# Group statistics moved into the filter network, and their rows kept in SBUF: one conv, attention and feed-forward block on one core

## The chip, the cores and the metric

The kernel runs on one core of one Trainium2 chip. The metric is the device time of one execution in microseconds (us), lower is better. The kernel before takes 5605.55 us, the median of three runs (5603.51 to 5610.34).

## The reference

Input x is 8 images of 56x56 tokens with 256 channels, float32. The block is a long-convolution layer, a linear attention and a feed-forward layer with a Haar transform. What this change touches is the front of the first layer:

```python
def _gn(v, G=32, eps=1e-05):              # group norm, 32 groups of 8 channels
    g = v.reshape(B_, H_, W_, G, C_ // G)
    m = jnp.mean(g, axis=(1, 2, 4), keepdims=True)
    s = jnp.var(g, axis=(1, 2, 4), keepdims=True)
    return ((g - m) / jnp.sqrt(s + eps)).reshape(v.shape)

def rpe_coeffs(...):                      # filter taps: a small network over 111 x 111 offsets
    t = coords @ rpe_in_w.T + rpe_in_b
    for i in range(3):
        t = relu(simple_rms(t)) @ rpe_h_w[i].T + rpe_h_b[i]
    return relu(simple_rms(t)) @ rpe_out_w.T + rpe_out_b

def _L0_conv_ref(x, ...):                 # called with _gn(x)
    shortcut = x
    xn = simple_rms(x)
    u, v = silu(xn @ W_u.T + b_u), silu(xn @ W_v.T + b_v)
    y = irfft2(rfft2(v) * rfft2(filter))
    return (u * y) @ W_o.T + b_o + shortcut

x = x + _L0_conv_ref(_gn(x), ...)
```

The filter does not depend on x, and the statistics of x (a mean and a variance for each image and group) do not depend on the filter.

## The kernel before, in words

The program is a row of phases. Each is a `Tools` block that owns its SBUF and PSUM tiles and semaphores and ends with a barrier of all engines (L149 to L153); the next phase's loads are issued only behind it. In a phase every engine has its own hand-written list of instructions, in the order of the code, and the engines meet at semaphores. SyncE (SP) issues the loads and stores. Tiles carry the phase's prefix: kr, st, pr, co, mx, at, ff.

**Filter network** (kernel_rows_phase, kr). All constants are loaded first, among them `coords`, 6 x 12544; TensorE, VectorE, ScalarE and GpSimd wait for all eleven loads, and TensorE for all four weight splits besides. Then come 14 steps of two halves u = 0, 1, each of four rows of offsets (448 points). A step has layers numbered n = 0 to 7 (n = 2 * layer + u). `deeper_layer` (TensorE) is six products, the block `mean` of 16 small matmuls for the layer before (L266), six products, and two bias products (L289). ScalarE squares (L348), rectifies (L352) and takes the root (L358); VectorE makes the low parts (`low_parts`, L429) and the scale rows (`next_scale`, L408 to L422). The tail of a step is eight rows m: output products, `kr_coef` (VectorE, L446), and `row_pass` (TensorE, L297) into the two PSUM banks `kr_row_ps`, which ScalarE copies out (L370). GpSimd only copies the points of the next step out of `coords` (L243).

**Statistics** (stats_phase, st). The 56 chunks of x (448 tokens each, tile 112 x 4 x 256) are loaded, turned by eight TensorE transposes (L797) into PSUM and measured by two VectorE bn_stats (L853). After each image come the two group means (L775, L779), the normalisers, four spreading matmuls that copy scale and shift along a row (L786), and a copy and seven stores that write the row of 512 values to `gn_rows` in DRAM, once for each chunk.

**Projection** (project_phase, pr). GpSimd clears four x tiles; then SP loads, for each chunk, two halves of x (56 rows x 4 KB each) and the chunk's row of `gn_rows`, broadcast to 128 partitions (256 KB). GpSimd multiplies and adds (L973, L976, `pr_gx`); ScalarE takes squares; TensorE turns (`front`, L993), projects (L135) and does the row transform (L1013). TensorE waits for all constants before the first `front`.

**Columns** (co) does the column transforms and is not touched. **Mix** (mix_phase, mx) loads x and the `gn_rows` row (224 KB) again for each chunk, and GpSimd again normalises (L1350, L1352) before TensorE turns the result (L1384). Attention (at) and feed-forward (ff) follow, untouched.

Of the kernel before, what the change touches and what calls it, by code (L numbers as in the profile page):

```python
# [165 lines left out]
def kernel_rows_phase(nc, d):  # L166

    with Tools(nc, "kr") as T:  # L170
# [14 lines left out]
        coords = T.sb("coords", [6, TAPS_PAD * TAPS_PAD])  # L185
# [9 lines left out]
        rows_out = [T.sb(f"rows_out{u}", [ROWS, RPE_ROWS, WIDE]) for u in range(2)]  # L195
        t_ps = [T.ps(f"t{u}", [128, 1024]) for u in range(2)]
# [4 lines left out]
        (consts_in, high_consts, low_consts, points_ready, layer_done, high_ready, low_ready, squared, mean_done, rooted,  # L201
         scaled, scale_split, scale_mixed, scale_ready, column_mm, inverted, coef_mm, coef_done, row_mm, row_out) = (T.sem(n) for n in (
             "consts_in", "high_consts", "low_consts", "points_ready", "layer_done", "high_ready", "low_ready", "squared",
# [8 lines left out]
        loads = [(raw_in, "rpe_in"), (coords, "coords"), (low_rows, "low_rows"), (own_row, "own_row"), (mean_ch, "mean_ch"),  # L212
                 (raw_h, "rpe_h"), (raw_bias, "rpe_bias"), (raw_out, "rpe_out"), (ident, "ident"), (out_bias, "rpe_out_b"),
                 (row_taps, "row_taps")]
# [9 lines left out]
        with nc.Block() as block:  # L224
            @block.sync
            def _(sp):
                for tile, name in loads:
                    sp.dma_start(tile[:], d[name]).then_inc(consts_in, 16)
                with sp.Fori(0, STEPS) as s:
                    for u in range(2):  # L230

                        sp.wait_ge(row_out, s * TAIL + RPE_ROWS * (u + 1))
                        sp.dma_start(d["kern_rows"][:, bass.ds((s * 2 + u) * RPE_ROWS, RPE_ROWS), :],
                                     rows_out[u][:]).then_inc(stored[u], 16)
# [4 lines left out]
            def _(pool):  # L239
                pool.wait_ge(consts_in, 16 * len(loads))  # L240

                def take_points(s, u):
                    nc.gpsimd.tensor_copy(points[u][:], coords[:, bass.ds((s * 2 + u) * RPE_CHUNK, RPE_CHUNK)]  # L243
                                          ).then_inc(points_ready, 1)

                for u in range(2):
                    take_points(0, u)
                with pool.Fori(1, STEPS) as s:
                    for u in range(2):
                        pool.wait_ge(layer_done, s * PER + (u + 1 - PER))  # L250
# [618 lines left out]
def project_phase(nc, d):  # L869

    with Tools(nc, "pr") as T:
# [52 lines left out]
        with nc.Block() as block:  # L924
            @block.sync
            def _(sp):
# [17 lines left out]
                for j in range(GROUP):  # L944
                    load(0, j)
# [1694 lines left out]
```

## Time and profile before

| what | value |
|---|---|
| median of three runs | 5605.55 us |
| the profiled execution | 5614.06 us, its span 5612.2 us |
| TensorE matmul | busy 5297.2 us, 94% of the span |
| VectorE | 3942.1 us, 70% |
| ScalarE | 2461.5 us, 44% |
| GpSimd | 2495.2 us, 44% |
| moved by DMA | 810.15 MB, mean 144 GB/s |
| mean granted clock of TensorE | 0.968 of full speed |

The profiled execution is 8.5 us above the median of the runs. The page of the profile gives busy time by engine and by fortieth of the span; the answers of the trace give single instructions with their start and duration (timeline), and sums over a stretch (windows). A matmul's end is modelled, so the pace of TensorE is read from start to start. The second row of the page's slices has TensorE below nine tenths in the first, fifth and sixth slices, where the phases kr, st and pr begin, and again at the later phase borders.

### The profile page before, as it was taken

How to read it: one execution, taken by the hardware profiler on the slowest of the kernel's cores; microseconds unless marked ns; L12 is line 12 of the kernel's file. 1: busy time of each engine (PE TensorE's matmuls, PEld its weight loads, DVE VectorE, ACT ScalarE, POOL GpSimd, SP SyncE). 2: the span in 40 equal slices, each digit the busy share in tenths (PEclk: the TensorE clock that was granted, in tenths of full speed). 3: DMA queues.
4: the chain of work that ended last, by engine and by line, in shares of the span. 5: the costliest groups of instructions: out<-in, count | busy, mean ns of one | idle time of the engine just before them, and what ended most of it. 6: DMA issues, size and time to landing. Idle time of an engine off the chain costs nothing. (4 is left out here: it accounts for less than half of the span.)

```text
span 5612.2 us, 90234 instructions
## 1 busy us (share of the span) xinstructions
PE 5297.2 (94%) x26964; PEld 3688.4 (66%) x26964; DVE 3942.1 (70%) x6109; ACT 2461.5 (44%) x4685; POOL 2495.2 (44%) x1385
## 2 busy tenths in 40 slices
PE   8999869998999999999998999999799999987999
PEld 5667545554555555555556777777676666665999
DVE  4555556665899999999995666676545555555787
ACT  4444238786334343443333555555532222210555
POOL 0000024442899999999995555555201111111332
PEclk9999879999999999999999999999899999997999
DMA  1111568887444444444446666666523333322443
GB/s 44 39 52 40 139 165 245 242 243 219 143 149 151 151 148 152 147 151 150 149 135 188 208 209 213 206 217 204 163 86 101 102 97 104 102 82 82 120 123 113
DMA packets 364270, 810.15 MB, mean 144 GB/s; under 512 B 45135, under 2 KB 149507, under 8 KB 354618
## 3 DMA queue, kind: packets, MB, share of 16 engines
q1 hardware_dynamic: 341648, 731.51, 44.3%
q10 hardware_dynamic: 22512, 77.20, 3.6%
q8 instruction: 66, 1.08, 0.1%
q14 instruction: 44, 0.36, 0.0%
HBM read 448.08 MB, written 360.49 MB: 144 GB/s over the span
## 5 line engine op out<-in xcount | busy, mean ns | idle before, releaser
L717 POOL TENSOR_TENSOR co_prod<-co_cross 111x512 f32<-111x512 f32 x448 | 850.2, 1898 | 0.0
L651 ACT ACTIVATE co_y_out<-co_y_ps 112x512 f32<-112x512 f32 x448 | 267.9, 598 | 927.6 <-PE co_y_ps L597 922.8
L714 POOL TENSOR_TENSOR co_prod<-co_direct 111x512 f32<-111x512 f32 x448 | 577.4, 1289 | 202.1 <-PE co_y_ps L597 115.4
L691 DVE TENSOR_TENSOR co_direct<-co_v_ps,co_spec 111x1024 f32<-111x1024 f32 x448 | 543.3, 1213 | 92.3 <-PE co_v_ps L135 87.8
L1917 POOL TENSOR_TENSOR at_t<-at_t,at_p_bias 112x1024 f32<-112x1024 f32 x56 | 134.2, 2409 | 976.1 <-DMA at_t<-t_tiles 976.1
L693 DVE TENSOR_TENSOR co_cross<-co_v_ps,co_spec 111x1024 f32<-111x1024 f32 x448 | 541.3, 1208 | 0.0
L135 PE MATMUL co_v_ps<-co_v_high,co_col_fwd_high 112*111 112x512 f32 x896 | 506.1, 565 | 1.4 <-DVE co_cross L693 1.4
L595 PE MATMUL co_y_ps<-co_prod,co_col_inv 111*112 111x512 f32 x896 | 458.2, 592 | 0.0
L597 PE MATMUL co_y_ps<-co_prod,co_col_inv 111*112 111x512 f32 x896 | 457.5, 592 | 0.1
L671 DVE TENSOR_TENSOR co_v_low<-co_v_in,co_v_high 112x1024 fp32r<-112x1024 f32 x224 | 372.4, 1662 | 0.1
L2081 ACT ACTIVATE at_qk_t<-at_bank_ps 128x448 f32<-128x448 f32 x224 | 121.8, 544 | 567.9 <-PE at_bank_ps L135 567.8
L135 PE MATMUL co_v_ps<-co_v_low,co_col_fwd_high 112*111 112x512 f32 x896 | 354.3, 395 | 0.0
L135 PE MATMUL co_v_ps<-co_v_high,co_col_fwd_low 112*111 112x512 f32 x896 | 349.2, 390 | 0.0
L1512 ACT ACTIVATE mx_mixed_high<-mx_turn_ps 128x448 fp32r<-128x448 f32 x224 | 122.0, 544 | 430.7 <-PE mx_turn_ps L1413 430.7
L597 PEld LDWEIGHTS co_y_ps<-co_prod,co_col_inv 111*112 111x112 f32 x896 | 156.0, 175 | 229.4 <-issue 212.3
L1148 DVE SCALAR_TENSOR_TENSOR pr_v_pre<-pr_v_ps,pr_inv,pr_v_bias 120x512 f32<-120x512 f32 x224 | 167.6, 748 | 155.9 <-PE pr_v_ps L135 150.6
L973 POOL TENSOR_TENSOR pr_gx<-pr_x_in,pr_gn 128x1024 f32<-128x1024 f32 x56 | 135.4, 2418 | 312.1 <-DMA pr_gn<-gn_rows 267.8
L2402 POOL TENSOR_TENSOR ff_base<-ff_t,ff_n 112x1024 f32<-112x1024 f32 x56 | 132.8, 2371 | 312.2 <-DVE ff_out L2563 280.9
L135 PE MATMUL mx_o_ps<-mx_w_o_high,mx_mixed_high 128*112 128x256 f32 x896 | 252.3, 282 | 3.5 <-DVE mx_mixed_low L1630 3.5
L135 PE MATMUL mx_o_ps<-mx_w_o_high,mx_mixed_low 128*112 128x256 f32 x896 | 252.1, 281 | 0.0
L243 POOL CAST kr_points<-kr_coords 6x448 fp32r (+1 forms) x28 | 15.6, 558 | 530.5 <-PE kr_t_ps L274 511.9
L135 PE MATMUL mx_o_ps<-mx_w_o_low,mx_mixed_high 128*112 128x256 f32 x896 | 250.7, 280 | 0.0
(267 smaller groups left out, 14107.8 us busy)
## 6 DMA issues: line engine op xcount, KB each, us to landing
v_rows<-pr_rows_out SPq DMA_DIRECT2D x56, 1792.0 KB
co_v_in<-v_rows SPq DMA_DIRECT2D x448, 224.0 KB
y_rows<-co_y_out SPq DMA_DIRECT2D x448, 224.0 KB
mx_y_in<-y_rows SPq DMA_DIRECT2D x224, 448.0 KB, 5.5
kern_rows<-kr_rows_out SPq DMA_DIRECT2D x28, 896.0 KB
st_x_in<-x SPq DMA_DIRECT2D x56, 448.0 KB, 11.4
pr_x_in<-x SPq DMA_DIRECT2D x112, 224.0 KB
mx_x_in<-x SPq DMA_DIRECT2D x56, 448.0 KB, 4.8
```

The source lines that it names most:

```text
L135: last = nc.tensor.matmul(out, weights[a], data[b], start=start and i == 0, stop=stop and i == len(passes) - 1)
L595: nc.tensor.matmul(y_ps[b % 2][:2 * SIDE, :], col_inv[:, 0, :], prod[b % 2][:, :WIDE], start=True, stop=False)
L597: nc.tensor.matmul(y_ps[b % 2][:2 * SIDE, :], col_inv[:, 1, :], prod[b % 2][:, WIDE:], start=False, stop=True).then_inc(inv_mm, 1)
L651: nc.scalar.activation(y_out[:, b, :], y_ps[b % 2][:2 * SIDE, :], ACT.Copy).then_inc(y_ready, 1)
L671: nc.vector.tensor_tensor(v[1][:, images, :], v_in[:, images, :], v[0][:, images, :].bitcast(F32), ALU.subtract).then_inc(low_v, 1)
L691: nc.vector.tensor_tensor(direct[b % 2][:], v_ps[b % 2][:POINTS, :], spec[i][:, :2 * WIDE], ALU.mult).then_inc(real_terms, 1)
L693: nc.vector.tensor_tensor(cross[b % 2][:], v_ps[b % 2][:POINTS, :], spec[i][:, WIDE:], ALU.mult).then_inc(multiplied, 1)
L714: nc.gpsimd.tensor_tensor(prod[b % 2][:, :WIDE], direct[b % 2][:, :WIDE], direct[b % 2][:, WIDE:], ALU.subtract).then_inc(real_ready, 1)
L717: nc.gpsimd.tensor_tensor(prod[b % 2][:, WIDE:], cross[b % 2][:, :WIDE], cross[b % 2][:, WIDE:], ALU.add).then_inc(combined, 1)
L973: nc.gpsimd.tensor_tensor(gx[j][:], x_in[j][:], gn[j][:, 0:1, :].to_broadcast([128, TILES, CH]), ALU.mult).then_inc(scaled, 1)
L1148: nc.vector.scalar_tensor_tensor(out=v_pre[t % 2][:], in0=v_ps[t % 2][:SPAN, :], scalar=inv[:SPAN, j % GROUP * TILES + t:j % GROUP * TILES ...
L1917: nc.gpsimd.tensor_tensor(t1[j % HELD][:], t1[j % HELD][:], p_bias[:].unsqueeze(1).to_broadcast([TILE, TILES, CH]), ALU.add).then_inc(t1_b ...
```

## The change

* stats_phase is gone. Its loads, transposes and bn_stats stand in the kr phase: five chunks a step, one behind each of the layers n = 2 to 6, in steps 0 to 10, the 56th chunk in step 11. They use the banks `kr_row_ps`, which the tail of the step uses otherwise. The aggregates are made in the tail of step 11, the group means and normalisers in step 12 for all images at once, and the spreading matmuls and copies of the eight rows in steps 12 and 13.
* `gn_rows` is an SBUF tile, 128 x 8 x 512, that lives from kr to mix. The DRAM tensor, its 56 stores and its 112 broadcast loads are gone.
* The points come in pieces of 6 x 448, two a step. The constants of kr are in three groups with a semaphore each (inputs, weights, tail), and each engine waits only for the group that it needs.
* In pr the first two chunks are loaded ahead of the constants, each as soon as its own tile is cleared; VectorE normalises chunk 0, GpSimd the others; ScalarE splits the weights and copies chunk 0 before it takes the squares of chunk 1; VectorE makes the first low part before the inverse.
* In mix the first x chunk is loaded ahead of the constants, and GpSimd does not wait for these to normalise.
* Loops: kr on TensorE, ScalarE and VectorE loops over 11 steps and has 3 written out (13 and 1 before); kr on SP and GpSimd, and the normalising on GpSimd in pr and mix, are written out in full.

```diff
-def kernel_rows_phase(nc, d):
+def kernel_rows_phase(nc, d, gn_rows):
+    PER_STEP = 5
-        coords = T.sb("coords", [6, TAPS_PAD * TAPS_PAD])
+        group_mean = T.sb("group_mean", [128, 128])
+        coords = [T.sb(f"coords{u}", [6, RPE_CHUNK]) for u in range(2)]
+        x_in = [T.sb(f"x_in{i}", [TILE, TILES, CH]) for i in range(PER_STEP)]
...
+        input_loads = [(raw_in, "rpe_in"), (low_rows, "low_rows")]
+        weight_loads = [(raw_h, "rpe_h"), (mean_ch, "mean_ch"), (raw_bias, "rpe_bias"), (own_row, "own_row"), (ident, "ident")]
+        tail_loads = [(raw_out, "rpe_out"), (out_bias, "rpe_out_b"), (row_taps, "row_taps"), (group_mean, "group_mean")]
+        X_LOOP = X_CHUNKS // PER_STEP
...
+                def load_x(s, i):
+                    if s:
+                        sp.wait_ge(turned, (s - 1) * PER_STEP + i + 1)
+                    sp.dma_start(x_in[i][:], d["x_tiles"][s * PER_STEP + i]).then_inc(x_loaded[i], 16)
...
+                def turn_chunk(s, i):
+                    pe.wait_ge(x_loaded[i], s * 16 + 16)
+                    if i:
+                        pe.wait_ge(measured, s * PER_STEP + i)
+                    if i < 2:
+                        pe.wait_ge(row_out, s * TAIL)
+                    for h in range(HALVES):
+                        for t in range(TILES):
+                            last = nc.tensor.transpose(row_ps[h][:, t * TILE:(t + 1) * TILE], x_in[i][:, t, h * 128:(h + 1) * 128],
+                                                       ident[:TILE, :TILE])
+                    last.then_inc(turned, 1)
...
                     for n in range(2, PER):
                         deeper_layer(s, n)
+                        between_layers(s, n)
...
                     for n in range(1, PER):
                         low_parts(s, n)
+                        between_layers(s, n)
                         next_scale(s, n)
...
+                def take_rows(b):
+                    dve.wait_ge(gn_mm, b + 1)
+                    nc.vector.tensor_copy(gn_rows[:, b, :], row_ps[b % 2][:]).then_inc(gn_ready, 1)
...
-def stats_phase(nc, d):
...
-                    sp.dma_start(gn[j][:].rearrange("p a c -> p (a c)"), d["gn_rows"][GROUP * s + j].to_broadcast([128, 2 * CH])
-                                 ).then_inc(loaded[j], 16)
...
-                sp.wait_ge(cleared, GROUP)
-                for j in range(GROUP):
+                for j in range(2):
+                    sp.wait_ge(cleared, j + 1)
                     load(0, j)
                 for tile, name in loads:
                     sp.dma_start(tile[:], d[name]).then_inc(consts_in, 16)
+                for j in range(2, GROUP):
+                    sp.wait_ge(cleared, j + 1)
+                    load(0, j)
...
+                dve.wait_ge(loaded[0], 32)
+                nc.vector.tensor_tensor(gx[0][:], x_in[0][:], scale0, ALU.mult).then_inc(scaled0, 1)
+                dve.wait_ge(scaled0, 1)
+                nc.vector.tensor_tensor(gx[0][:], gx[0][:], shift0, ALU.add).then_inc(gx_ready, 1)
```

TensorE at the end of layer n = 2 of a kr step, before (kr_t0_ps belongs to half 0; the two bias products end the layer):

```order
L135 MATMUL kr_t0_ps<-kr_rect0_high,kr_w_h_low 128x448
L287 ISA
L289 MATMUL kr_t0_ps<-kr_scale_rows0,kr_bias_rows_both 128x448 x2
L280 ISA
L135 MATMUL kr_t1_ps<-kr_rect1_high,kr_w_h_high 128x448
```

and after:

```order
L135 MATMUL kr_t0_ps<-kr_rect0_high,kr_w_h_low 128x448
L386 ISA
L388 MATMUL kr_t0_ps<-kr_scale_rows0,kr_bias_rows_both 128x448 x2
L309 ISA
L316 MATMUL kr_row0_ps<-kr_ident,kr_x_in0 128x112 x4
L316 MATMUL kr_row1_ps<-kr_ident,kr_x_in0 128x112 x4
L379 ISA
L135 MATMUL kr_t1_ps<-kr_rect1_high,kr_w_h_high 128x448
```

The eight transposes of one chunk stand between the bias products of one layer and the first product of the next.

VectorE around the same layer, after; before, the same rows stood there without the BN_STATS and their ISA rows:

```order
L541 SCALAR_TENSOR_TENSOR kr_rect_low<-kr_t_ps,kr_rect_high 128x448
L549 ISA
L557 ISA
L557 BN_STATS kr_stats<-kr_row_ps 128x6
L557 ISA
L557 BN_STATS kr_stats<-kr_row_ps 128x6
L513 REGISTER_ALU
L522 SCALAR_TENSOR_TENSOR kr_scale<-kr_scale,kr_root 128x112
L527 CAST kr_scale_high<-kr_scale 128x112
L528 REGISTER_ALU
L529 SCALAR_TENSOR_TENSOR kr_scale_both<-kr_scale_high,kr_low_rows,kr_scale 128x112
L534 TENSOR_TENSOR kr_scale_rows<-kr_scale_both,kr_own_row 128x448
```

The two bn_stats stand between the low parts and the scale of a layer.

VectorE at the start of pr, before:

```order
L1176 TENSOR_TENSOR pr_w_v_low<-pr_raw_v,pr_w_v_high 128x1024
L1178 TENSOR_SCALAR pr_guarded<-pr_root 128x8
L1180 RECIPROCAL pr_inv<-pr_guarded 128x8
L1140 TENSOR_TENSOR pr_x_t_low<-pr_xt_ps,pr_x_t_high 128x480 x2
L1148 SCALAR_TENSOR_TENSOR pr_v_pre<-pr_v_ps,pr_inv,pr_v_bias 120x512 x2
```

and after:

```order
L1207 TENSOR_TENSOR pr_gx<-pr_x_in,gn_rows 128x1024
L1209 TENSOR_TENSOR pr_gx<-pr_gx,gn_rows 128x1024
L1211 TENSOR_TENSOR pr_w_v_low<-pr_raw_v,pr_w_v_high 128x1024
L1170 TENSOR_TENSOR pr_x_t_low<-pr_xt_ps,pr_x_t_high 128x480 x2
L1214 TENSOR_SCALAR pr_guarded<-pr_root 128x8
L1216 RECIPROCAL pr_inv<-pr_guarded 128x8
L1178 SCALAR_TENSOR_TENSOR pr_v_pre<-pr_v_ps,pr_inv,pr_v_bias 120x512 x2
```

Two operations on chunk 0 come first, and the low part of the turned chunk no longer stands behind the inverse.

## Rows read from the trace of the kernel before

**Rows 1.** Windows: stretch, us, busy us (count) by engine, clock, DMA share, GB/s.
```profile
45.00:630.70 585.70, 582.83 (x3813) 402.19 (x3811) 323.37 (x702) 284.04 (x540) 13.43 (x24) 1.00 0.13 42
641.00:760.50 119.50, 81.38 (x544) 68.89 (x544) 80.29 (x192) 1.62 (x8) 0.00 (x0) 0.80 0.95 210
800.00:1380.00 580.00, 579.87 (x2646) 343.61 (x2644) 380.86 (x607) 460.08 (x1057) 243.78 (x102) 1.00 0.79 237
```

**Rows 2.** Timeline (start us, duration us, instruction, idle before): borders of the st phase.
```profile
636.09 0.37 SPq L757 DMA_DIRECT2D st_ident<-ident  x1
...
641.09 3.30 PE L797 MATMUL st_x_ps<-st_ident,st_x_in 112*128 112x112 f32 x16 [11.47 <-DMA st_x_in<-x]
...
760.54 3.62 POOL L965 MEMSET pr_x_in<- 128x1024 f32 x4 [214.03 <-POOLq L153]
```

**Rows 3.** Timeline: one layer of a kr step.
```profile
554.25 0.35 PEld L266 LDWEIGHTS kr_ms_ps<-kr_square,kr_mean_ch 128*32 128x32 f32 x16 [0.30 <-ACT kr_square L348]
...
554.53 1.16 DVE L429 SCALAR_TENSOR_TENSOR kr_rect_low<-kr_t_ps,kr_rect_high 128x448 fp32r<-128x448 f32 x2 [0.87 <-ACT kr_rect_high L352]
...
555.60 0.27 DVE L410 SCALAR_TENSOR_TENSOR kr_scale<-kr_scale,kr_root 128x112 f32<-128x112 f32 x1
...
556.53 0.62 DVE L422 TENSOR_TENSOR kr_scale_rows<-kr_scale_both,kr_own_row 128x448 fp32r<-128x448 f32 x1
...
557.80 0.35 PEld L266 LDWEIGHTS kr_ms_ps<-kr_square,kr_mean_ch 128*32 128x32 f32 x16 [0.30 <-ACT kr_square L348]
```

**Rows 4.** Timeline of TensorE: a turned chunk and a spread row in st.
```profile
663.69 0.98 PE L797 MATMUL st_x_ps<-st_ident,st_x_in 112*128 112x112 f32 x8 [0.96 <-DMA st_x_in<-x]
664.51 0.65 PE L786 MATMUL st_row_ps<-st_ident,st_scale 128*128 128x128 f32 x4
...
665.54 0.98 PE L797 MATMUL st_x_ps<-st_ident,st_x_in 112*128 112x112 f32 x8
```

**Rows 5.** Timeline of TensorE: a turned chunk inside a full stream, in pr.
```profile
1005.95 1.04 PE L993 MATMUL pr_xt_ps<-pr_ident,pr_gx 120*128 120x120 f32 x8
1006.75 0.47 PE L135 MATMUL pr_v_ps<-pr_w_v_high,pr_x_t_high 128*120 128x512 f32 x1
```

**Rows 6.** The tile st_stats: duration ns min/median/max, first and last start.
```profile
L853 DVE BATCH_NORM_STATS2 st_stats<-st_x_ps x112: 612/616/633, 642.9 to 748.1; 128x6 f32<-128x448 f32 x112
```

**Rows 7.** Timeline: start of the kr phase.
```profile
18.98 0.41 ACT L340 ACTIVATE kr_w_in_high<-kr_raw_in 6x256 fp32r<-6x256 f32 x1 [16.95 <-DMA kr_row_taps<-row_taps]
...
21.41 1.04 ACT L343 ACTIVATE kr_w_out_high<-kr_raw_out 128x1024 fp32r<-128x1024 f32 x1
...
25.84 0.92 ACT L348 ACTIVATE kr_square<-kr_t_ps 128x896 f32<-128x896 f32 x1 [3.39 <-PE kr_t_ps L274]
...
28.75 0.74 PE L135 MATMUL kr_t_ps<-kr_rect_high,kr_w_h_high 128*128 128x448 f32 x1
```

**Rows 8.** DMA between 14 and 19 us.
```profile
DMA packets 294, 0.33 MB, mean 65 GB/s; under 512 B 129, under 2 KB 177, under 8 KB 294
```

**Rows 9.** Timeline: start of the pr phase.
```profile
771.31 2.34 POOL L973 TENSOR_TENSOR pr_gx<-pr_x_in,pr_gn 128x1024 f32<-128x1024 f32 x1 [7.16 <-DMA pr_gn<-gn_rows]
...
782.97 1.06 ACT L1111 ACTIVATE pr_w_v_high<-pr_raw_v 128x1024 fp32r<-128x1024 f32 x1 [0.20 <-DMA pr_ident<-ident]
...
784.06 2.56 DVE L1176 TENSOR_TENSOR pr_w_v_low<-pr_raw_v,pr_w_v_high 128x1024 fp32r<-128x1024 f32 x1 [28.08 <-ACT pr_w_v_high L1111]
...
790.43 0.75 PE L135 MATMUL pr_v_ps<-pr_w_v_high,pr_x_t_high 128*120 128x512 f32 x1 [5.58 <-issue]
```

**Rows 10.** Timeline: start of the mx phase.
```profile
2969.33 1.23 DVE L1722 TENSOR_TENSOR mx_w_u_low<-mx_raw_u,mx_w_u_high 128x1024 fp32r<-128x1024 f32 x1 [6.20 <-ACT mx_w_u_high L1592]
...
2981.28 2.37 POOL L1350 TENSOR_TENSOR mx_gx<-mx_x_in,mx_gn 112x1024 f32<-112x1024 f32 x1 [4.88 <-DMA mx_gn<-gn_rows]
...
2986.40 0.93 PE L1384 MATMUL mx_turn_ps<-mx_ident,mx_gx 112*128 112x112 f32 x4
```

**Rows 11.** Timeline of TensorE in st: a chunk turned at the lower clock.
```profile
671.29 1.75 PE L797 MATMUL st_x_ps<-st_ident,st_x_in 112*128 112x112 f32 x8 [0.42 <-DMA st_x_in<-x]
```

More of the change, by code:

```diff
@@ L239, in _ @@
             def _(pool):
[L240 removed]
                 def take_points(s, u):
[L243 to L248, printed above, removed]
+                    pool.wait_ge(coords_in[u], 16 * (s + 1))
+                    if s:
+                        pool.wait_ge(layer_done, s * PER + (u + 1 - PER))
+                    nc.gpsimd.tensor_copy(points[u][:], coords[u][:]).then_inc(points_ready, 1)
+                for s in range(STEPS):
                     for u in range(2):
[L250 removed]
                         take_points(s, u)
@@ new lines, in spread_rows @@
+                def spread_rows(b):
+                    pe.wait_ge(chain, SHIFT)
+                    if b >= 2:
+                        pe.wait_ge(gn_ready, b - 1)
+                        pe.wait_ge(row_out, (X_LOOP + 2) * TAIL)
+                    for i, col in enumerate((gn_scale, gn_shift)):
+                        for h in range(HALVES):
+                            at = (i * HALVES + h) * 128
+                            last = nc.tensor.matmul(row_ps[b % 2][:, at:at + 128], col[:, h, b:b + 1].to_broadcast([128, 128]),
+                                                    ident[:], start=True, stop=True)
+                    last.then_inc(gn_mm, 1)
@@ L1356, in residual @@
                     pool.wait_ge(gx_ready, g + 1)
-                    if not first:
+                    if first:
+                        pool.wait_ge(consts_in, 16 * (len(loads) + 2))
+                    else:
                         pool.wait_ge(t1_ready, s * 4 + (u - 1) * 2 + SLOTS)
@@ L1368, in _ @@
                 residual(0, 1, first=True)
-                with pool.Fori(1, PAIRS - 1) as s:
+                for s in range(1, PAIRS - 1):
                     normalise(s, 1)
@@ L2584, in program @@
     scratch("kern_rows", (ROWS, TAPS_PAD, WIDE))
-    scratch("gn_rows", (chunks, 1, 2 * CH))
     scratch("inv_cols", (chunks // 2, 128, 2 * TILES))
@@ L2598, in program @@
     d["out"] = d["result"].rearrange(flat).rearrange("(g t p) c -> g p t c", t=TILES, p=TILE)
-    for phase in (kernel_rows_phase, stats_phase, project_phase, columns_phase, mix_phase, attention_phase, ffn_phase):
-        phase(nc, d)
+    with nc.sbuf_tensor("gn_rows", [128, BATCH, 2 * CH], F32) as gn_rows:
+        kernel_rows_phase(nc, d, gn_rows)
+        project_phase(nc, d, gn_rows)
+        columns_phase(nc, d)
+        mix_phase(nc, d, gn_rows)
+    attention_phase(nc, d)
+    ffn_phase(nc, d)
 def kernel(**inputs):
```

346 lines of the change are left out of this document (170 added, 176 removed).

## The prediction

> **What bounds the kernel now.** I read the slices of the page first, to find where TensorE is not full, then windows over the stages that the change touches, then the timeline at their borders. The windows [rows 1] show three different cases. In kr TensorE is busy 582.83 of 585.70 us at full clock (2.4 GHz), while VectorE works 323 us and the DMA engines 13% of the time: TensorE sets the pace, and the DMA queues and nearly half of VectorE are free. In st it is the other way round: DMA share 0.95 at 210 GB/s, TensorE 81 of 119.5 us and mostly waiting for the next chunk (the row of [rows 2] at 641.09 waits for `st_x_in`). In pr TensorE is full again, 579.87 of 580, at full clock. So the change takes a stretch bound by loads and puts it under a stretch bound by TensorE. The loads become free there, the transposes do not.
>
> **The statistics phase goes.** Its first instruction is at 636.09 us and the next phase's first at 760.54 [rows 2], the one SP's first load and the other GpSimd's first clear behind the same kind of barrier. That is 124.4 us off, with a barrier, the waiting for the first load, the closing chain of normalisers and the stores of `gn_rows` all inside.
>
> **What TensorE gets in kr.** Turning a chunk takes 0.82 us from start to start (663.69 to 664.51, [rows 4]), in a full stream 0.80 with 120 columns instead of 112 [rows 5]. Changing from products to another kind of matmul costs something too: the block of means has 0.30 us of idle weight loading before it [rows 3], and between bias products and next layer there is no such change today. No row shows this very change, so I bound it by 0 and by 0.5 us a chunk (such a gap on entering and some of one on leaving), and take 0.2, nearer to the lower end because pr has the same change without a visible loss: 1.0 us x 56 chunks = 56 us (45 to 73). A spread row takes 1.03 us (664.51 to 665.54, [rows 4]), eight of them 8.2 us; two group means, each no longer than the half of such a row, 1 us. Together 65 us, all on the path, since TensorE is full.
>
> **What VectorE gets in kr.** A layer lasts 3.55 us on TensorE (554.25 to 557.80, [rows 3]) and becomes 4.55 us. VectorE has 1.16 us of low parts and 1.55 us of scale work in it (555.60 to the end of 556.53 + 0.62, [rows 3]), and gets 2 x 0.616 us of bn_stats [rows 6]: 3.94 of 4.55 us, so it should still fit. Behind the bn_stats stand the scale, the next low parts and the next bias product, which have about a layer of slack. The tight one is the new wait: the next chunk may be turned only when the last one is measured, since both use the same two banks. Low parts start about 1.4 us after a layer's last product (554.53 is 0.28 behind the block of means, which has six products ahead of it), end at 2.6, the bn_stats at about 3.9, and the next turn is due at 4.55. Slack 0.6 us: no cost. The copies of the rows (one a layer) and the aggregates in the tail are smaller than a chunk's bn_stats and hide the same way. ScalarE gets one small root.
>
> **Queues.** SP now waits for a turned chunk before each x load, and the stores of `kern_rows` stand behind these waits. The last chunk of a step is turned at n = 6, and the store waits for a row of the tail anyway, so nothing is late. Each x load has a whole step before it is needed, some 45 us, where a load lands within 5 us (636.09 to 641.09, two small constants included, [rows 2]). Points have at least as long. GpSimd's copies are two small ones a step. All of this costs nothing; if a load were late, TensorE would wait for it in the turn.
>
> **Start of kr.** Now everything lands at 18.98 us, ScalarE splits the four weights, the last of them at 21.41, the first square is at 25.84 and the first deep product at 28.75 [rows 7], 9.8 us after landing. After the change only the last split (1.04 us) stands between the landing of the tail group and the first square, since the first layer is done by then; from square to product stays 2.91 us. That is 4.1 us after landing instead of 9.8: 5.7 us saved. When the tail lands is open: between 14 and 19 us only 0.33 MB moved, in small packets at 65 GB/s [rows 8], and the row tables that are last now are still in the last group. I take 1.2 us earlier for the 294 KB of coordinates that left the queue (bounds: 0.5 later, 5 earlier). Sum 6.9 us (5 to 11).
>
> **Start of pr.** The weights and constants land at 782.97, behind four chunks with their broadcast rows, and products start at 790.43 [rows 9]. By the shapes the queue carried 4 x 704 KB + 0.9 MB from the end of the clears (760.54 + 3.62, [rows 2]) on, in 18.8 us, about 200 GB/s. After: two chunks of 448 KB and 0.9 MB, 9 us, and the queue starts 2.7 us earlier because it waits for one of the four clears: constants at about 771. Then turn, copy, low part, about 4.7 us: products at 776.0, 14 us earlier. The new work on VectorE is two passes over 128 x 1024. The same kind of pass took 1.23 us with GpSimd idle [rows 10] and 2.56 us beside GpSimd [rows 9], so 2.5 to 5.1 us, and it ends before the constants land either way if chunk 0 lands in 5 us. The range of this term is 10 to 16 us.
>
> **Rest of pr, and mix.** The broadcast loads that go were beside a full TensorE: nothing. At the start of mix, TensorE turns the second chunk at 2986.40, right behind GpSimd's work on it, which began at 2981.28 when its row had landed [rows 10]. 448 KB less in front of it are 2 us at the 210 GB/s of [rows 1]. The first products come some 4 us earlier, but then wait for that chunk: 2 us (0 to 4).
>
> **Sum.** -124.4 + 65 - 6.9 - 14 - 2 = -82 us. The profiled execution took 5614 us and would take 5532; the median of the runs is 8.5 us lower, so 5523.5 us. About 0.2% (11 us) is what a measurement of this kernel can tell from no change.
>
> **A rule against the change.** The windows with transposes show both levels of the clock: pr, which turns a chunk between its products, has 1.00, and st, where TensorE waits between chunks, has 0.80; there a chunk's eight transposes took 1.75 us at one place [rows 11] and 0.98 at another [rows 4]. The Trainium skill ("TensorE: Matmul & The Clock Gate", Part 4: PE-mode transpose) says that transpose mode does not count as busy for the clock in the way that matmuls do. By that rule five interruptions a step could cost kr its full clock (the third rival below); the full clock of pr speaks against it for short groups.
>
> **The rivals.**
> * *VectorE or the two banks set the pace.* If the register work and waits around the bn_stats, which no row shows, eat the slack, TensorE waits for `measured` before each turn. With 5.1 us a layer that is 0.55 x 55 = 30 us more, 5554 us. If turn and bn_stats stood wholly in line, 1.23 x 56 = 69 us more, 5592 us. For it: 0.6 us of slack in a hand-timed chain. Against it: 3.94 of 4.55. 10%.
> * *The starts give little.* The tail of small packets stays and GpSimd holds VectorE in pr: 8 us instead of 23, 5538 us. 9%, inside the range.
> * *Slower: the clock falls in kr.* Place: the eleven steps with chunks. Price: a step is 43 us (28.75 to 630.7 in 14) and would take up to twice that at 1.2 GHz, 43 us each; from two steps on it eats the 82 us, all eleven would make it 6000 us. For it: st's 0.80 [rows 1]. Against: in st TensorE idled a third of the time, in kr it will not. 3%.
> * *The statistics are not hidden at all* (loads too late, turns waiting for DMA): as in the first rival; 1%, since the queue is at 13%.
>
> **How the numbers follow.** The forecast, 5523.5 us, has 77%, with a range of its own of 5503 (turns at 0.8 us, starts at their best) to 5548 us (turns at 1.3 us, starts at their worst). That holds the second rival and part of the first, so it is the range. Faster by over 0.2% is everything but the clock and the fully serial case: 0.95; within 0.2%, 0.02; slower 0.03.
>
> **What would show it.** The first clear of pr should come at about 636 + 65 - 7 = 694 us, with TensorE full at clock 1.00 up to there; a step with chunks 5 us longer than 43; turns without idle time before them released by `kr_stats`; DMA near 130 GB/s there. Products of pr should start 15 to 17 us after its first clear, not 30. Wrong would be: a TensorE wait on the bn_stats in kr, a clock below 1.00 there, or steps of over 51 us.

## The result, and the profile after

The changed kernel takes 5512.68 us (median of 4 runs, 5506.79 to 5516.2), the kernel before 5606.46 us on the same chip (4 runs, 5603.51 to 5610.34): ratio 0.9837, 95% interval 0.9824 to 0.9849, so 94 us faster. The forecast was 5523.5 us in a range of 5503 to 5548. The profiled execution took 5516.2 us with a span of 5514.4 us, against 5532 forecast for it. The page of the changed kernel, busy time by engine, then TensorE and its granted clock in 40 slices:

```profile
PE 5263.6 (95%) x26936; PEld 3667.2 (67%) x26936; DVE 3927.7 (71%) x6061; ACT 2458.8 (45%) x4678; POOL 2490.1 (45%) x1383
...
PE   8999899997999999999989999999799999987999
...
PEclk9999999998999999999999999999899999998999
```

The first window of the next view is the stretch of the kr phase with chunks in it, the second its end (columns as in [rows 1]):

```profile
45.00:570.00 525.00, 521.29 (x3587) 370.65 (x3585) 324.48 (x693) 237.31 (x450) 11.62 (x22) 1.00 0.26 80
570.00:676.00 106.00, 105.18 (x675) 73.69 (x673) 59.89 (x136) 46.47 (x88) 1.06 (x2) 1.00 0.14 44
```

TensorE is as full as in [rows 1], at clock 1.00 in both windows, and the DMA share has only doubled. So the statistics are hidden behind TensorE in all but their transposes. The timeline of one layer shows how (start us, duration us, instruction):

```profile
311.24 0.59 PE L365 MATMUL kr_ms_ps<-kr_square,kr_mean_ch 128*32 128x112 f32 x16
...
311.88 1.15 DVE L557 BATCH_NORM_STATS2 kr_stats<-kr_row_ps 128x448 f32 x2
...
312.95 0.26 DVE L522 SCALAR_TENSOR_TENSOR kr_scale<-kr_scale,kr_root 128x112 f32<-128x112 f32 x1
...
313.08 0.57 PE L388 MATMUL kr_t_ps<-kr_scale_rows,kr_bias_rows_both 128*128 128x448 f32 x2
...
313.48 0.93 PE L316 MATMUL kr_row_ps<-kr_ident,kr_x_in 112*128 112x112 f32 x8
...
314.19 0.45 PE L135 MATMUL kr_t_ps<-kr_rect_high,kr_w_h_high 128*128 128x448 f32 x1
...
315.58 0.47 PE L365 MATMUL kr_ms_ps<-kr_square,kr_mean_ch 128*32 128x112 f32 x9
```

A layer with a chunk goes from 311.24 to 315.58, 4.34 us; without one it was 3.55 [rows 3]. In none of the 56 turns does TensorE stand idle before it. The last chunk's bn_stats end at 313.03, 0.45 us before the next turn at 313.48.

The border of the phases and the start of pr, from the timeline (idle time before in brackets):

```profile
681.98 3.62 POOL L995 MEMSET pr_x_in<- 128x1024 f32 x4 [92.23 <-POOLq L153]
...
687.32 1.22 DVE L1207 TENSOR_TENSOR pr_gx<-pr_x_in,gn_rows 128x1024 f32<-128x1024 f32 x1 [13.31 <-DMA pr_x_in<-x]
688.58 1.22 DVE L1209 TENSOR_TENSOR pr_gx<-pr_gx,gn_rows 128x1024 f32<-128x1024 f32 x1
...
692.15 1.06 ACT L1139 ACTIVATE pr_w_v_high<-pr_raw_v 128x1024 fp32r<-128x1024 f32 x1 [0.60 <-DMA pr_ident<-ident]
...
693.24 2.33 DVE L1211 TENSOR_TENSOR pr_w_v_low<-pr_raw_v,pr_w_v_high 128x1024 fp32r<-128x1024 f32 x1 [3.43 <-ACT pr_w_v_high L1139]
...
696.80 0.75 PE L135 MATMUL pr_v_ps<-pr_w_v_high,pr_x_t_high 128*120 128x512 f32 x1 [2.77 <-issue]
```

pr begins at 681.98 instead of 760.54 [rows 2], 78.6 us earlier. Its first product comes 14.8 us after that instead of 29.9 [rows 9]. Then the gap between the two kernels stays the same for 3200 us: 93.6 us at pr's first product, 94.1 us at the last product `mx_u_ps` of mix. The other 3.7 us of the span's 97.8 come behind mix, where the code is unchanged.

The start of kr (timeline):

```profile
17.05 1.06 ACT L452 ACTIVATE kr_w_out_high<-kr_raw_out 128x1024 fp32r<-128x1024 f32 x1 [5.93 <-DMA kr_group_mean<-group_mean]
18.01 0.90 ACT L457 ACTIVATE kr_square<-kr_t_ps 128x896 f32<-128x896 f32 x1
...
21.00 0.74 PE L135 MATMUL kr_t_ps<-kr_rect_high,kr_w_h_high 128*128 128x448 f32 x1
```

The first deep product is at 21.00 instead of 28.75 [rows 7]. So the kr phase from its first deep product to pr's first clear grew by 124.45 + 7.75 - 78.56 = 53.6 us.

### The profile page after: what moved, and what is told of

It is laid out like the page before. It is cut to its first block and busy times, and to the rows that moved or that the text cites. A ratio compares the mean times of both kernels' runs of the same rounds, so it can differ in the third digit from the quotient of the medians.

```text
span 5514.4 us, 88804 instructions
## 1 busy us (share of the span) xinstructions
PE 5263.6 (95%) x26936; PEld 3667.2 (67%) x26936; DVE 3927.7 (71%) x6061; ACT 2458.8 (45%) x4678; POOL 2490.1 (45%) x1383
## 5 line engine op out<-in xcount | busy, mean ns | idle before, releaser
L1395 POOL TENSOR_TENSOR mx_resid<-mx_x_in,mx_o_bias 112x1024 f32<-112x1024 f32 x56 | 133.2, 2379 | 319.0 <-DVE mx_t L1677 319.0
L297 POOL CAST kr_points<-kr_coords 6x448 fp32r<-6x448 f32 x28 | 15.0, 558 | 574.3 <-DMA kr_coords<-coords 574.3
L1005 POOL TENSOR_TENSOR pr_gx<-pr_x_in,gn_rows 128x1024 f32<-128x1024 f32 x55 | 133.3, 2424 | 300.0 <-DMA pr_x_in<-x 299.9
```

## The experiments

Eleven kernels ran, each the changed kernel with one edit, or several where said. Where only a span is given, it is that of a single execution; three of the kernels were run 4 or 5 times. "Deep product" is the first product of a deeper layer in kr, "clear" the first clear that opens pr or mix.

**What a chunk costs TensorE.** The forecast had 0.2 us a chunk for changing to transposes and back.

```
-                        for t in range(TILES):
+                        for t in range(TILES // 2):
                             last = nc.tensor.transpose(row_ps[h][...
-                        last = nc.vector.bn_stats(at[h], row_ps[h][:, :CHUNK])
+                        last = nc.vector.bn_stats(at[h], row_ps[h][:, :CHUNK // 2])
```

Half of the points are left out of the statistics here.

> Leaves out half of the statistics: only four of a chunk's eight transposes, and bn_stats over 224 of 448 columns, so the statistics are those of half the tokens. A step with five chunks lasts 46.98 us in the changed kernel and 42.86 before: 0.82 us a chunk. Theory A (a transpose costs its own columns and entering and leaving transposes costs nothing): 0.41 us a chunk, a step of 44.9 us, kr 23 us shorter. Theory B (my 0.2 us of switching is there, and the transposes are cheaper than I took them): 0.2 + 0.31 us a chunk, a step of 45.4 us.

Span 5485.1 us (time 5486.89). The timeline of TensorE in two successive layers, blocks of means, bias products and turns:

```profile
301.02 0.59 PE L365 MATMUL kr_ms_ps<-kr_square,kr_mean_ch 128*32 128x112 f32 x16
...
302.87 0.57 PE L388 MATMUL kr_t_ps<-kr_scale_rows,kr_bias_rows_both 128*128 128x448 f32 x2
...
303.27 0.55 PE L316 MATMUL kr_row_ps<-kr_ident,kr_x_in 112*128 112x112 f32 x4
...
304.99 0.59 PE L365 MATMUL kr_ms_ps<-kr_square,kr_mean_ch 128*32 128x112 f32 x16
```

A layer takes 3.97 us, against 4.34 with eight transposes and 3.55 with none [rows 3]: 0.42 us for the first four, 0.37 for the next four. A fixed price for the change of kind would leave the first four much dearer; 0.05 us is left for it. By whole steps it is nearly the same: 45.10 us here, 46.98 in the changed kernel, 42.86 before, so 0.45 us a chunk for the first half and 0.38 for the second, with 0.07 left. The price of a chunk is that of its eight transposes, 0.82 us by whole steps, with the change of kind in it. Theory A had 44.9 us for the step, theory B 45.4; 45.10 lies between them, nearer to A.

**Whether VectorE has slack.** Each bn_stats is made twice, the first into a tile that nobody reads:

```
                     for h in range(HALVES):
+                        nc.vector.bn_stats(spare[:, h, :], row_ps[h][:, :CHUNK])
                         last = nc.vector.bn_stats(at[h], row_ps[h][:, :CHUNK])
```

> Each chunk is measured twice (four bn_stats instead of two, the first two into a spare tile), 1.23 us more for VectorE in each layer with a chunk: 5.2 us of work in a layer of 4.34. Theory (VectorE has 0.4 to 0.6 us of slack a layer and TensorE waits for nothing but the banks): the next turn now waits for the measuring, a layer lasts 4.9 to 5.2 us, a step 50 to 51 us, kr 32 to 45 us longer, with TensorE idle ahead of the turns and kr_stats as the releaser. Rival (the slack of the low parts and the scale, about a layer, takes it up): a step of 47 to 48 us.

Span 5526.1 us (time 5527.92), a step 48.62 us: 1.6 us more in five layers, of 5.4 us more work. TensorE, blocks of means, and then VectorE in the same stretch:

```profile
330.94 0.59 PE L366 MATMUL kr_ms_ps<-kr_square,kr_mean_ch 128*32 128x112 f32 x16
...
333.46 0.78 PEld L317 LDWEIGHTS kr_row_ps<-kr_ident,kr_x_in 112*128 112x128 f32 x8 [0.49 <-DVE kr_stats L559]
333.46 0.98 PE L317 MATMUL kr_row_ps<-kr_ident,kr_x_in 112*128 112x112 f32 x8
...
335.61 0.59 PE L366 MATMUL kr_ms_ps<-kr_square,kr_mean_ch 128*32 128x112 f32 x16
```

```profile
330.12 1.16 DVE L542 SCALAR_TENSOR_TENSOR kr_rect_low<-kr_t_ps,kr_rect_high 128x448 fp32r<-128x448 f32 x2
331.19 0.62 DVE L558 BATCH_NORM_STATS2 kr_spare<-kr_row_ps 128x6 f32<-128x448 f32 x1
331.73 0.61 DVE L559 BATCH_NORM_STATS2 kr_stats<-kr_row_ps 128x448 f32 x1
...
334.78 1.15 DVE L542 SCALAR_TENSOR_TENSOR kr_rect_low<-kr_t_ps,kr_rect_high 128x448 fp32r<-128x448 f32 x2
```

VectorE now works without a gap and its cycle is 4.66 us (330.12 to 334.78), which is also TensorE's layer (330.94 to 335.61, 4.67). One bn_stats costs 0.54 us from start to start, so without the two extra ones the cycle is 3.6 us of work against a layer of 4.34. The weight load of the turn waits for `kr_stats`, as the theory said: 55 of the 56 turns do so here, 30.8 us in all, and none in the changed kernel. So the wait for the banks, the forecast's first rival, exists and begins to cost once VectorE's work exceeds the layer. Neither expectation hit the size (steps of 50 to 51 or 47 to 48 us): there is slack of 0.7 us a layer, 0.3 of the 1.07 us doubled does not fit.

**The start of kr.** In the next kernel everything waits for the last load, as in the kernel before, the coordinates still loaded by the step:

```
 def _(pe):
+    pe.wait_ge(inputs_in, ...)
+    pe.wait_ge(weights_in, ...)
+    pe.wait_ge(tail_in, ...)
+    pe.wait_ge(low_consts, 4)
-    pe.wait_ge(low_consts, 1)
```

and likewise for ScalarE and GpSimd.

> The changed kernel, but in kr TensorE, VectorE, ScalarE and GpSimd wait for all three groups of constants (TensorE for the four splits too) before anything else, as before the change; the points still come by the step. First deep product: 21.0 us in the changed kernel, 28.75 before. Theory (5.7 us are the splits and the first layer done ahead, 2 us the coordinates that left the queue): 26.8 us. Rival (the smaller load is all of it): 21 to 22 us. Other rival (only the grouping counts): 28.5 us. The rest of kr keeps its length.

Deep product at 27.7 us instead of 21.0, pr's clear at 688.3 instead of 682.0: 6.3 to 6.7 us are the order of waits and splits, and the 1.1 us left to the kernel before (28.75) would be the smaller load. The theory had 26.8 us, the second rival 28.5. One run does not settle between them: in the eight kernels that have the changed kernel's start of kr the deep product came at 19.3 to 21.2 us. With this old order it came at 27.5 to 27.7 in two kernels, so most of the saving is the order. The span was 5513.0, no longer than the changed kernel's, mostly because mix and attention, untouched by the edit, took 1.6 and 5.1 us less in this run; the last section has the spread of attention. That is why the phase borders are compared here and not the ends.

The opposite edit goes further: no engine waits for the tail group before the w_out products of step 0, and the bias and w_h splits stand where they are first needed.

```
-                pe.wait_ge(tail_in, 16 * len(tail_loads))
-                pe.wait_ge(low_consts, 4)
+                pe.wait_ge(low_consts, 3)
                 over_steps(pe, step)
...
+                    if isinstance(s, int) and s == 0:
+                        pe.wait_ge(tail_in, 16 * len(tail_loads))
+                        pe.wait_ge(low_consts, 4)
                     for m in range(TAIL):
```

> One step further than the change: in kr the squares, rectified and low parts of the first layer are made before the weights land, TensorE starts the deep layers as soon as the weights group is split, and the output weights (tail group, landing at 17.0 us) are split only in the sixth layer of step 0, which is written out. Theory: weights land at 8.9 us, two splits in line are 3.4 us: first deep product at 12.5 us instead of 21.0, and the first clear of pr 8.5 us earlier. Rival (step 0 then waits for its x chunks or for the tail group): the deep product comes at 12.5 us, but TensorE stands idle later in step 0 and less than 4 us are left.

```profile
12.85 1.11 PE L374 MATMUL kr_t_ps<-kr_points,kr_w_in_both 6*128 6x448 f32 x2 [3.33 <-DVE kr_bias_rows_both L631]
13.88 0.74 PE L135 MATMUL kr_t_ps<-kr_rect_high,kr_w_h_high 128*128 128x448 f32 x1
```

Deep product at 13.9, pr's clear 8.1 us earlier (673.9), span 5503.6 (time 5505.42). So in the changed kernel the wait for the tail group and the splits before the first square still stood on the path, with 7.1 us by this pair of profiles and 5.4 to 7.3 against the 19.3 to 21.2 us above. Both texts had 12.5 us for the deep product; TensorE did not lose the gain again later in step 0, as the rival said.

**The start of pr.** The order of the kernel before is put back (all four clears, then all four chunks, then the constants; GpSimd normalises chunk 0), while the rows stay on chip:

```
-                for j in range(2):
-                    sp.wait_ge(cleared, j + 1)
-                    load(0, j)
+                sp.wait_ge(cleared, GROUP)
+                for j in range(GROUP):
+                    load(0, j)
                 for tile, name in loads:
```

> The changed kernel with the start of pr in its old order: SP waits for all four clears, loads four chunks and then the constants, GpSimd normalises chunk 0 too, ScalarE and VectorE have their old order. The broadcast loads stay away. In the changed kernel the first product of pr starts 14.8 us after the first clear (29.9 before). Theory (order of loads and work): constants now lie behind four chunks of 448 KB instead of two, so the first product comes 27 us after the first clear (2.5 us less than before, for the 1 MB of broadcast loads at 200 GB/s would be 5, of which the chain through GpSimd takes back half), and the whole kernel takes 12 us more. Rival (the missing broadcast loads are what saved it): the first product comes at 16 to 18 us, 2 us more at most.

```profile
697.80 1.86 PE L1017 MATMUL pr_xt_ps<-pr_ident,pr_gx 120*128 120x120 f32 x8 [24.32 <-DMA pr_ident<-ident]
...
699.63 1.04 ACT L1135 ACTIVATE pr_w_v_high<-pr_raw_v 128x1024 fp32r<-128x1024 f32 x1
...
700.70 2.87 DVE L1200 TENSOR_TENSOR pr_w_v_low<-pr_raw_v,pr_w_v_high 128x1024 fp32r<-128x1024 f32 x1 [28.39 <-ACT pr_w_v_high L1135]
703.50 2.30 DVE L1202 TENSOR_SCALAR pr_guarded<-pr_root 128x8 f32<-128x8 f32 x1
...
707.39 0.75 PE L135 MATMUL pr_v_ps<-pr_w_v_high,pr_x_t_high 128*120 128x512 f32 x1 [7.73 <-issue]
```

The clear was at 680.3, the first product 27.1 us later; the theory had 27. The later loads are the larger part of it: the constants were there 17.5 us after the clear (first turn, 697.80) instead of 10.2, which is 7.3 of the 12.3 us. The other 5.0 lie behind them: ScalarE splits w_v only after the squares of two chunks, and VectorE makes the low part only after the guard, which took 2.30 us beside GpSimd. The edit moves loads, chunk 0 and the order of work on two engines at once, and no run separates these. Of the 15.1 us gained at this place 12.3 are thus the order (with chunk 0 on VectorE), and the 2.8 left are put down to the broadcast loads that left the queue; the next experiment measures these by themselves. pr itself takes 586 us from first to last product either way. Span 5523.1 (time 5524.87).

**The broadcast rows.** They are loaded again beside each chunk, in pr and in mix, with nobody reading them:

```
+                    sp.dma_start(gn[j][:]..., d["x_pairs"][GROUP * s + j].to_broadcast([128, 2 * CH])
+                                 ).then_inc(loaded[j], 16)
```

> The changed kernel with a broadcast load of 512 values for each chunk put back in pr (256 KB) and mix (224 KB), from x and unused, in the old places of the queue, and waited for. Theory (TensorE is full in both phases, the loads are hidden): the starts of pr and mix lose what lies in front of their constants and second chunk, 2 to 3 us in pr and 0 to 2 in mix; between starts and ends both phases keep their length to 1 us; the kernel takes 2 to 5 us more. Rival (keeping the rows on chip is worth more than its starts, by less traffic beside the stores): 10 us more or above, with longer steps in pr or mix.

5516.91 us (5512.26 to 5520.66; ratio 0.984, 0.982 to 0.986), not to be told from the changed kernel. pr's first product comes 2.0 us later after the clear, mix's 1.1 us, and pr's length stays (584.7 us). Keeping the rows on chip is worth what they cost in a start queue, 3 us in all, and nothing that these runs could show beside a full TensorE.

**The start of mix.** The order of before (weights, then each chunk with its inverse rows):

> The changed kernel with the start of mix in its old order: the constants ahead of the first x chunk, GpSimd waits for them. In the changed kernel the first product starts 18.3 us and the turn of the second chunk 24.5 us after the first clear of the phase; before 19.3 and 24.5. Theory (both are held by what the queue has to move before the second chunk, which is the same in either order): first product at 18 to 19.5 us, turn of the second chunk at 23 to 24.5 us, no loss, perhaps a gain of 1 us. Rival (the new order saved 2 us, and something else ate it): turn of the second chunk at 26 to 27 us.

First product 20.5 us after the clear instead of 18.3, turn of the second chunk at 25.6 instead of 24.5, and 1047.4 us from clear to last product instead of 1045.5; span 5517.8. The theory (18 to 19.5 and 23 to 24.5 us) missed both, the rival (26 to 27) is nearer. A single pair of runs does not prove it, but the other profiles have the same starts: in the seven kernels with the new order the first product came 17.3 to 18.5 us after the clear and the second turn at 22.1 to 24.5, in the three with the old one (this one, all three starts old, and the kernel before, which has the broadcast loads besides) 19.1 to 20.5 and 24.4 to 25.6. The first products do not overlap, so the new order gains about 1.7 us on the mean there, and about 1 us at the second turn. From clear to last product it is 1043.9 to 1047.0 against 1046.4 to 1047.4. In the changed kernel's own profile the second chunk is still late, turned 24.5 us after the clear as before ([rows 10] and 2961.9 for the clear). So I put both x chunks ahead of everything but the constants:

```
-                for u in range(2):
-                    if u:
-                        load_x(0, u, first=True)
-                    load_inv(0, u, first=True)
+                load_x(0, 1, first=True)
+                for u in range(2):
+                    load_inv(0, u, first=True)
```

> The changed kernel with one edit: in the mix phase both x chunks are loaded ahead of the first y and inverse rows (before, the second chunk stands behind ten other loads; in the changed kernel it landed late enough that GpSimd normalised it 19.5 us after the phase's first clear and TensorE turned it at 24.5 us). Theory (the second turn waits for the queue in front of its chunk): the second turn comes 2 to 4 us earlier, the first product stays within 1 us of 18.3 us after the first clear or is up to 1 us later, and from the first clear to the last product the phase takes 1042 to 1044 us instead of 1045.4. Rival (the loads only change places, the y rows are then what comes last): 1045 to 1047 us and the first product a microsecond or two later. Both: nothing outside the phase, whole span within 5 us of 5514.

No gain: 1047.7 us from clear to last product, first product at 21.0, second turn at 25.9 (span 5514.9). The rows of VectorE and GpSimd in that start:

```profile
2879.80 2.79 POOL L1383 TENSOR_TENSOR mx_gx<-mx_x_in,gn_rows 112x1024 f32<-112x1024 f32 x1 [2.21 <-DMA mx_x_in<-x]
2882.67 3.21 POOL L1385 TENSOR_TENSOR mx_gx<-mx_gx,gn_rows 112x1024 f32<-112x1024 f32 x1
```

```profile
2880.31 3.36 DVE L1757 TENSOR_TENSOR mx_w_o_low<-mx_raw_o,mx_w_o_high 128x1024 fp32r<-128x1024 f32 x1
```

The second chunk is there some 7 us earlier, counted from the clear, and GpSimd takes it up just when VectorE splits w_o. That split took 1.22 us in the changed kernel, with GpSimd idle, and 3.36 here, and TensorE's first turn waits for it. This is the rival's outcome and a little more (first product 2.7 us later), by a path that neither text named.

**All three starts old.** The three edits together, in 3 rounds:

> The statistics in the filter network and the rows on chip alone: the starts of kr, pr and mix all in their old order (the edits of the three runs on them together). Theory (parts add up): against the changed kernel +5.8 us in kr, +12 in pr, 0 in mix; against the kernel before -98 + 18 = -80 us or, from the part itself, -124.4 + 53.6 - 2 - 2.5 = -75 us, ratio 0.986 to 0.987. Rival (the starts hide in each other, since a phase that starts later finds its clock or its queue in another state): less than 10 us above the changed kernel.

5533.32 us (5523.17 to 5542.77; ratio 0.9866, 0.9841 to 0.9891). At the borders: deep product 27.5, clear of pr 687.9, product 27.1 us after it, span 5533.1, 18.7 above the changed kernel. The parts add up (6.5 + 12.3 + about 1 = 20). Against the kernel before on the same chip (5605.32 us) the statistics in kr and the rows on chip alone gave 72 us, where the expectation had 75 to 80; the three starts are the rest.

**pr prepared inside kr.** pr's first product came 14.8 us after the first clear, while kr's end had 6.8 us in which three engines stood and only the last store ran. So the first four chunks and pr's constants are loaded in step 12 of kr, GpSimd normalises the four chunks after the last normaliser row, and behind the steps:

```
+                nc.scalar.activation(pre["w_v"][0][:], raw_v[:], ACT.Copy).then_inc(pr_high, 1)
+                for j in range(2):
+                    act.wait_ge(first_ready, j + 1)
...
+                        last = nc.scalar.activation(junk[:, t, :], gx_first[j][:, t, :], ACT.Square, ...
```

> The changed kernel with the start of the project phase moved into the end of the filter network: its first four x chunks, w_v, the bias and the matrices are loaded in step 12 of 14, GpSimd clears and normalises those four chunks after the last group normaliser row is copied, ScalarE and VectorE split w_v and make the first two chunks' squares and inverses while the last filter rows are stored (6.8 us in which the three engines stood in the changed kernel). Theory: the project phase has its first product 3 to 5 us after its start instead of 14.8 us after the first clear, its length from first to last product stays 586 us, the filter network grows by under 1 us, and all that follows is 10 to 12 us earlier: span about 5503. Rival 1 (the work at the end of the filter network outlasts the stores: GpSimd's eight operations, beside VectorE's, come after the last row is stored): the phase start moves back by 2 to 6 us and the gain is 5 to 9 us, span about 5507. Rival 2 (1.5 MB of loads in step 12 and GpSimd's port use slow the last two steps of the filter network): its last row 3 or more us later.

```profile
675.35 0.60 ACT L505 ACTIVATE kr_rows_out<-kr_row_ps 112x512 f32<-112x512 f32 x1 [0.50 <-PE kr_row_ps L425]
675.85 1.05 ACT L518 ACTIVATE pr_w_v_high<-kr_raw_v 128x1024 fp32r<-128x1024 f32 x1
675.97 0.32 SPq L300 DMA_DIRECT2D kern_rows<-kr_rows_out  x1
...
680.76 0.20 DVE L670 RECIPROCAL pr_inv<-pr_guarded 128x8 f32<-128x8 f32 x1
682.11 1.49 PEld L1043 LDWEIGHTS pr_xt_ps<-pr_ident,pr_gx 120*128 120x128 f32 x8 [7.63 <-POOLq L1018]
...
686.35 0.78 PE L135 MATMUL pr_v_ps<-pr_w_v_high,pr_x_t_high 128*120 128x512 f32 x1 [2.38 <-DVE pr_x_t_low L1178]
```

The last filter row is copied at 675.35 (675.22 in the changed kernel), the prepared work ends at 681.0, inside the time of the last store, and the first product is at 686.35, 4.2 us after the phase opens: 10.5 us earlier than 696.80. Span 5503.8 (time 5505.63). The starts went as the theory said, and rival 1 fell. But 1.2 of the 10.5 us are a deep product that came earlier in this run (19.77); counted from it, the gain is 9.2 us. For kr itself grew by 1.4 us from deep product to last row (655.6 against 654.2), where the theory had under 1. GpSimd's clears of the four tiles, which run in step 0, show why:

```profile
23.65 4.52 DVE L555 TENSOR_SCALAR kr_scale<-kr_root 128x112 f32<-128x112 f32 x1 [0.93 <-ACT kr_root L490]
24.47 3.62 POOL L317 MEMSET pr_x_in<- 128x1024 f32 x4
...
31.64 0.98 PE L339 MATMUL kr_row_ps<-kr_ident,kr_x_in 112*128 112x112 f32 x8 [1.46 <-DVE kr_stats L592]
```

A scale row on 128 x 112 elements that took 0.22 us at 21.38 in the changed kernel lasts 4.52 us, until the last clear is done, and TensorE waits for VectorE before a bias product (0.56 us) and before a turn (1.46). That is the slowing by GpSimd that rival 2 named, in the first step and not in the last two, and with 1.4 us instead of 3.

**Together.** The kr start, pr prepared in kr, and both x chunks first in mix, 5 rounds:

> The three start edits together: the filter network's start with each weight waited for where it is used (8.1 us gained alone), the project phase prepared inside the filter network (10 to 12 us expected) and both x chunks first in the mix phase (0 to 2 us expected). Theory (the starts are separate, nothing overlaps them): span 20 us (17 to 22) under that of the changed kernel, so 5494, time about 5493 (5488 to 5498), ratio to the kernel before 0.980. Rival (they share the DMA queue or the engine time, so that parts are lost): 5500 or more.

5495.89 us (5493.62 to 5498.33), ratio 0.9807 (0.9793 to 0.982): 16.8 us under the changed kernel and 109 us under the one before on the same chip (5604.59). The time is in the range expected (5488 to 5498), the gain at its lower end (17.8 us by the span, 5496.6, where 17 to 22 were expected). The intervals of the two ratios do not overlap. pr's first product is at 678.6, 18.2 us earlier: 7.2 at the deep product and 10.9 from there on. The latter is 1.7 more than in the run before, as here the clears (25.96 to 29.65) fell beside other rows of VectorE and kr kept its length (653.9 us from deep product to last row). The mix edit gave nothing here either: 1045.2 us from clear to last product, with the split of w_o again at 3.36 us.

## Why the prediction was right, point by point

- **What bounds.** Right: TensorE full at clock 1.00 in kr before and after, st a stretch of loads. With 4 us of transposes in each 47 us step the granted clock stayed at its upper level (1.00, 2.4 GHz). The Trainium skill's rule in "TensorE: Matmul & The Clock Gate", Part 4: PE-mode transpose, that transpose mode does not count as busy for the clock, is neither confirmed nor refuted by this: among products, transposes in groups of eight did no harm. The first clear of pr was put at 694 us and came at 682, by the 11.4 us of the term on kr below and 0.9 of its start.
- **The phase that goes**, -124.4 us: as read.
- **TensorE in kr**, +65 forecast, +53.6 measured. This is the term that was mis-sized. "Changing from products to another kind of matmul costs something too [...] and take 0.2": the half turn leaves 0.05 to 0.07 us for it, and that is inside the 0.82 us that a chunk cost, the sum's bound below. 1.0 was taken, so 0.18 x 56 = 10 us is nearly the whole error. A spread row cost 0.89 us (a layer with one 4.44, without 3.55) instead of 1.03, another 1 us. The sum 56 x 0.82 + 8 x 0.89 = 53.0 leaves 0.6 us for the group means.
- **VectorE.** Right that it fits, with 0.45 us between its last bn_stats and the next turn where 0.6 was forecast, though the layer came out 0.2 us shorter. Its work was put too high: 3.94 us as a sum of durations, 3.6 by the doubled run, since neighbouring rows overlap by some 0.08 us each. The first rival (5554 or 5592 us) needed the contrary; with the bn_stats doubled its wait appears.
- **Queues.** Right: an x load lands in 3.7 us (median of 56), no turn waits for one. The rate of 130 GB/s named as a sign was wrong: 80 GB/s. Five chunks of 448 KB in 47 us are 49 GB/s, and the 42 of [rows 1] spread over the longer step 38, so 87 at the most, which I had not worked out.
- **Start of kr**, -6.9 forecast, -7.75 measured: the tail landed 1.9 us earlier (17.05 instead of 18.98), where 1.2 was taken, and from there it is 3.95 us to the deep product (4.1). Over the eight kernels with this start (19.3 to 21.2 us) the gain against the one profile of before is 7.5 to 9.4.
- **Start of pr**, -14 forecast, -15.1 measured. Constants 10.2 us after the clear (10.5 forecast), products 4.65 us after them (4.7). VectorE's two passes took 1.22 us each, the lower bound, as GpSimd had no chunk yet.
- **Start of mix**, -2 forecast. The size is about right (1 to 2 us), the reason only in part. In this pair of profiles the second chunk's turn did not come earlier, still 24.5 us after the clear; over all kernels it came about 1 us earlier. What changed clearly is the first product, 18.3 us after the clear instead of 19.3, about 1.7 us over all kernels. The forecast had 4 us there, all but 2 of them lost again in the wait for the chunk.
- **What is left.** Forecast for the profiled execution 5532, measured 5516.2, 15.8 less. 11.4 are kr, 0.9 and 1.1 the two starts; mix's 2 showed as 0.5 in this pair of profiles (1.5 the other way). The other 3.7 us arose behind mix, in unchanged code, and lie within the spread given below.

The second rival (starts give little, 5538 us) fell with the two starts, the clock rival with 1.00 in kr.

## What to carry to other kernels

Work bound by loads can be laid under a stretch bound by TensorE, and its price is then only its own matmuls: price an inserted block of transposes by start-to-start time in a full stream and add next to nothing for the change of kind (here under 0.1 us). Once phases stand end to end, look at each start: wait for every weight where it is first used, load first what the first instruction needs, and prepare the next phase in the time in which the last store lands. Loads that ran beside a full TensorE here gained nothing by going and cost nothing by staying that four runs could show; in the queue of a start they cost 1 to 3 us. When GpSimd work is moved to another place, look at what VectorE does beside it there.

## What the runs showed of the hardware that I had not expected

- **Eight fp32 transposes of 112 columns inside a stream of products cost 0.82 us, four 0.42 to 0.45**: a switching price of 0.05 to 0.07 us at the most, and a granted clock of 1.00 throughout.
- **GpSimd beside VectorE slows even tiny operations.** The split of 128 x 1024 with both inputs on chip took 1.22 us with GpSimd idle (mix of the changed kernel), 2.33 in pr of the changed kernel, 2.87 and 3.36 in the runs with the pr order of before and with both x chunks first. In the first of these a VectorE operation on 128 x 8 elements took 2.30 us beside GpSimd (0.17 with GpSimd idle, in the run with pr prepared in kr), and one on 128 x 112 lasted 4.52 us, through four clears in a row. Rows of VectorE that read PSUM kept their time: the low part `pr_x_t_low` took 1.21 us beside GpSimd in the changed kernel and 1.22 with GpSimd idle in the same other run. Meanwhile GpSimd's own passes took up to 3.2 instead of 2.34 us. What a start saves on a load it can lose in this way.
- **Unchanged code varies by several us between executions.** From ScalarE's first split of weights (`at_w_qk_high`) to the last `at_qk_t` copy the attention phase took 974.7 us before, 972.6 in the changed kernel, and 967.2 to 974.4 in the eleven other kernels, all with the same code there. For effects under 5 us the borders of the stage are the measure, not the end of the program.
